# Selective scan: the product with C on GpSimd by block of 512 instead of two blocks, in half of the units

## The reference

```python
def step(hst, ins):
    dt_t, B_t, C_t, x_t = ins
    dA = jnp.exp(dt_t[:, :, None] * A)
    hst = hst * dA + (dt_t * x_t)[:, :, None] * B_t[:, None, :]
    y_t = jnp.einsum('bds,bs->bd', hst, C_t)
    return (hst, y_t)
```

## Time and profile before

| what | value |
|---|---|
| median of 3 runs | 3693.93 us (3689.43 to 3694.01) |
| profiled execution, its own time | 3693.79 us |
| its span, first to last instruction | 3691.7 us |
| TensorE busy | 3177.4 us (86%) |
| ScalarE busy | 3172.4 us (86%) |
| DVE busy | 3007.0 us (81%) |
| GpSimd busy | 2572.3 us (70%), 1578 instructions |
| mean granted TensorE clock | 0.964 of full speed |
| chain that ended last, shares | ScalarE 59%, TensorE 23%, GpSimd 11%, DVE 4% |

### The profile page before, as it was taken

The page is one execution under the profiler, slowest core; times in us unless marked ns, Lnnn a source line. Parts: engine busy times, 40 slices in busy tenths (PEclk is TensorE's granted clock), DMA queues, the critical chain, the costliest instruction groups (busy, mean ns, idle before and its releaser), DMA issues.

```text
span 3691.7 us, 55673 instructions
## 1 busy us (share of the span) xinstructions
PE 3177.4 (86%) x20898; PEld 2324.0 (63%) x20898; DVE 3007.0 (81%) x2909; ACT 3172.4 (86%) x5100; POOL 2572.3 (70%) x1578
## 2 busy tenths in 40 slices
PE   7778898888878887888798889878888898999999
PEld 3676777677767776777687777767777432222244
DVE  2797898899889988988898899889999478888341
ACT  3799999999999999999999999999999235777721
POOL 0699998899999988998998899999879100000000
PEclk9899999999999999999999999999999998999999
DMA  2011111111112111111111111112111043121000
GB/s 93 29 52 54 47 52 51 43 55 50 53 47 78 52 54 47 51 49 48 57 52 53 45 55 51 49 46 69 52 41 52 12 103 69 18 35 18 1 6 17
DMA packets 65196, 175.90 MB, mean 48 GB/s; under 512 B 13697, under 2 KB 17537, under 8 KB 64673
## 3 DMA queue, kind: packets, MB, share of 16 engines
q1 hardware_dynamic: 64930, 172.36, 15.3%
HBM read 162.83 MB, written 9.44 MB: 47 GB/s over the span
## 4 chain that ended last, share of the span: by engine, by line
ACT 59%; PE 23%; POOL 11%; DVE 4%; issue 1%; DMA 0%; SPq 0%; DVEq 0%; POOLq 0%; ACTq 0%
ACT arena L852 27%; ACT arena L859 26%; PE psum L1182 10%; POOL arena L642 10%; PE psum L1482 3%; PE psum L1471 3%; PE psum L1446 2%; DVE row_max L1135 2%; PE psum L1390 2%; PE psum L1395 1%; POOL arena L622 1%; PE psum L1415 1%; POOL carry L638 1%; DVE arena L1088 1%; ACT arena L725 1%
## 5 line engine op out<-in xcount | busy, mean ns | idle before, releaser
L642 POOL TENSOR_TENSOR arena<-arena 128x1024 f32<-128x1024 f32 x1024 | 2424.5, 2381 | 171.7 <-DVE arena L1088 127.9
L1390 PE MATMUL psum<-ident,arena 128*128 128x128 f32 x8192 | 1278.3, 280 | 323.7 <-ACT arena L852 274.6
L1390 PEld LDWEIGHTS psum<-ident,arena 128*128 128x128 f32 x8192 | 972.5, 143 | 602.1 <-ACT arena L852 385.5
L852 ACT ACTIVATE arena<-arena,bT 128x512 f32<-128x512 f32 x2048 | 1310.9, 721 | 24.2 <-PE psum L1390 24.1
L1395 PE MATMUL psum<-ident,arena 128*128 128x128 f32 x8192 | 1261.7, 278 | 80.3 <-POOL arena L642 79.4
L1088 DVE TENSOR_TENSOR_SCAN arena<-arena,psum 128x512 f32<-128x512 f32 x1024 | 1179.9, 1204 | 169.5 <-PE psum L1390 100.6
L859 ACT ACTIVATE arena<-arena,a_neg 128x512 f32<-128x512 f32 x2048 | 1312.2, 722 | 1.6 <-DVE arena L1088 1.4
L1088 DVE TENSOR_TENSOR_SCAN arena<-arena,carry,psum 128x512 f32<-128x512 f32 x1024 | 1225.1, 1260 | 95.4 <-ACT arena L859 58.4
L1395 PEld LDWEIGHTS psum<-ident,arena 128*128 128x128 f32 x8192 | 971.8, 143 | 119.2 <-POOL arena L642 118.9
L1182 PE MATMUL psum<-arena 128*128 128x512 f32 x1472 | 710.3, 606 | 14.1 <-DVE arena L968 6.2
L1182 PEld LDWEIGHTS psum<-arena 128*128 128x128 f32 x1472 | 259.9, 195 | 209.2 <-issue 200.1
(11 more groups left out here) (109 smaller groups left out, 1079.6 us busy)
## 6 DMA issues: line engine op xcount, KB each, us to landing
arena<-bc_dram SPq DMA_DIRECT2D x256, 512.0 KB, 3.6
arena<-qk_dram SPq DMA_DIRECT2D x96, 128.0 KB
qk_dram<-arena SPq DMA_DIRECT2D x12, 512.0 KB, 4.9
arena<-in_x SPq DMA_DIRECT2D x4, 512.0 KB, 10.8
arena<-in_up_w SPq DMA_DIRECT2D x1, 2048.0 KB, 12.2
out_xT<-arena SPq DMA_DIRECT2D x8, 256.0 KB, 2.2
arena<-in_mlp_w SPq DMA_DIRECT2D x3, 512.0 KB, 6.4
arena<-in_fwd_xproj_w SPq DMA_DIRECT2D x1, 1280.0 KB, 10.1
```

The source lines that it names most:

```text
L642: pool.tensor_tensor(h_now[:, f:f + NI // 2], h_now[:, f:f + NI // 2], c_row, ALU.mult)\
L852: act.activation(uT[:, w % 2, c], dtxT[:, u % 2, c], ACT.Copy, scale=bT[:, u % 2, c, st:st + 1])\
L1390: o = pe.transpose(dst[:, c * P:(c + 1) * P], uT[:, w % 2, c, f * P:(f + 1) * P], ident[:, :])
```

## The change

In the units with `hi` = 1 GpSimd multiplies each block by itself: four operations of 128x512 a state, each behind its own scan. The units with `hi` = 0 keep their copies and their two operations. Since a state now has two or four products, a function `products(w, f)` counts how many are done when block f of state w is. TensorE waits for this count ahead of every sum, where it waited ahead of every second one, and the loads of C and the first state of a unit wait for the count of a whole state.

```diff
+        def products(w, f):
+            full = {0: 2, 1: NI}
+            before = sum(DS * full[unit(u)[2]] for u in range(w // DS))
+            n = full[unit(w // DS)[2]]
+            return before + w % DS * n + (f + 1 if n == NI else f // 2 + 1)
...
                     if p >= 2:
-                        sp.wait_ge(s["prod_done"], 4 * (p - 1))
+                        sp.wait_ge(s["prod_done"], products(2 * p - 3, NI - 1))
...
-                    for k in range(2):
+                    if hi:
+                        for f in range(NI):
+                            pool.wait_ge(s["scan_done"], NI * w + f + 1)
+                            pool.tensor_tensor(h_now[:, f], h_now[:, f], c_rows[:, p % 2, w % 2], ALU.mult)\
+                                .then_inc(s["prod_done"], 1)
+                    for k in range(0 if hi else 2):
                         f = k * NI // 2
                         pool.wait_ge(s["scan_done"], NI * w + f + NI // 2)
...
             def reduce_state(w, f):
-                if f % 2 == 0:
-                    pe.wait_ge(s["prod_done"], 2 * w + f // 2 + 1)
+                pe.wait_ge(s["prod_done"], products(w, f))
...
                 if c == 0:
                     pe.wait_ge(s["skip_w_ready"], 2 * NI)
-                    pe.wait_ge(s["prod_done"], 2 * (w + 1))
+                    pe.wait_ge(s["prod_done"], products(w, NI - 1))
```

## The result

The changed kernel takes 3699.76 us in the median of 19 runs (3696.26 to 3700.85), the kernel before 3692.24 us in 19 runs beside them (3687.57 to 3694.66). The ratio is 1.0020, with a 95% interval of 1.0013 to 1.0027: slower, by 7.5 us. The forecast was no change, 3693.4 us. The profiled executions took 3693.79 and 3699.74 us, with spans of 3691.7 and 3697.7.

The account below looks back on a forecast made before the run. ScalarE was taken to set the pace in the changed units, with GpSimd close behind. Terms -1.45 + 0 + 1.0 + 0.1 = -0.35 against the profiled 3693.79 us gave 3693.4, range 3687 to 3704.

Parts of the forecast that it names:

- The price of a block: GpSimd's product of 128x512 in a chain: 1.23 us, bounds 1.17 and 1.30; 4.92 a state against 4.67.
- Full stretches of the changed units: Four changed units: GpSimd needs 319 us of a unit's 342 and stays under ScalarE's total; cost 0.
- The product dt times xs: Units 1, 3, 5, behind state 48 on GpSimd: it starts 1.0 us earlier, ScalarE's three idle times go; -1.45 us.
- From there to the unit's end: GpSimd's last 60 blocks of units 1, 3, 5 end 2.8 us later; 2.0 us of slack left; cost 0.
- Starts of changed units: Units 1, 3, 5, 7, state 0: four blocks take 4.92 where two halves take 4.67; +1.0 us.
- End of unit 7: GpSimd's last 56 blocks end 0.6 us later, four transposes instead of eight save 0.5; +0.1 us.
- The rival "slower": GpSimd becomes the late one, from 1.26 us a block; mild form 3701 to 3706, full 3726; chance 0.13.
- The rival "faster": Finer sums free TensorE sooner, 3.95 us idle at changed units' starts goes; at most 16 us, 3678; chance 0.05.

Follow-up runs that it names:

- the late wait: Changed kernel with the first state's wait for its products moved behind the skip term and made block by block: 3681.68 us, 0.9976 of the kernel before.
- its two relatives: The late wait in the kernel before, with no state split: 3691.74 us; the late wait with blocks of 512 only up to state 48: 3685.68 us.

## Why the prediction was wrong

**The price of a block** was right: 1.23 us forecast, (74.22 - 1.29) / 59 = 1.236 measured; 1296 ns for one operation against 1268 in attention. The prediction's estimate of 1.17 us, from the Trainium skill's 4497 ns (GPSIMD Engine Reference, Performance versus the Vector engine), was too low here; that figure is for an addition of 2048 elements, and a product of 2048 took 4542 ns in this trace.

**Full stretches of the changed units** were right: unit 3 takes 342 us as before, with 13 us more of GpSimd's time hidden behind ScalarE. GpSimd did not become the bound.

**The product dt times xs** had the right size: it starts about 0.9 us earlier within unit 3 (1414.86, where the unit itself starts 0.3 earlier), and ScalarE's 0.87, 0.34 and 0.24 us ahead of state 52 are gone, -1.45. The reason was incomplete, as the run with state 48 alone shows: it gave no gain.

**From there to the unit's end, cost 0**, is the step that failed. Its arithmetic held: the last product was to end at 1493.3 and ends at 1493.6, and the last sum, for which I had found 2.0 us of slack, is on time. But I followed the delay only to this one waiter. GpSimd's next work is state 0 of the next unit, 2 x 2.58 us from 1493.5 to 1498.7, and TensorE's first sum wants all of it at 1497.7. I had described exactly this wait, for the starts of the other units, and had not looked for it here. By the threshold of the forecast a block had to be over 1.26 us; it decided at less. In the profile ScalarE's idle time at the starts of units 2, 4 and 6 went from 0.96, 0.95 and 0.95 to 2.12, 3.51 and 3.32: **+6.1 us**, nearly the whole 6.0 us by which the span grew. That blocks from state 49 alone cost the full amount and blocks up to state 48 nothing in sum, and that enough idle work on GpSimd (eight memsets) does the same without any block, is shown by runs. How the 6.1 us divide into the late sum and TensorE's clock is shown in part only. The prediction had no term for the clock. It had also put the last product some 5 us behind the last scan; it ends 6.8 behind (1493.6, the scans of unit 3 at 1486.8), since the last scans come 0.9 us earlier than before.

**Starts of changed units, +1.0 us.** The waits for GpSimd grew at three of the four (0.52 to 0.79 us in unit 1, 0.36 to 0.80 in unit 5, 0.35 to 0.47 in unit 7; 0.38 instead of 0.51 in unit 3). ScalarE's idle time is 2.2 us more in sum, of which 2.0 are in unit 5, where the clock is low for longer. At the other three it changed by +0.27, -0.12 and +0.06, where +0.25 each was forecast: one of three came out, and the term as a whole was short by the clock at unit 5.

**End of unit 7, +0.1 us.** Measured +0.6: the last product ends 3.5 us behind the last scan (2.4 before), since the lag of earlier states had not run out, and TensorE's last group saves 0.43.

The sum -1.45 + 6.1 + 2.2 + 0.6 is 7.5, and the span grew by 6.0. Of the rest 0.99 us is idle time of ScalarE ahead of state 52 of unit 0, which is gone too; about 0.5 us is not accounted for. The rival "slower" named the right engine and the right stretch, the chain without a gap, but its price came from the last sums and from a threshold that did not decide. The rival "faster" said that the idle time at the start of a changed unit could go; it does not by the change. Once the wait is late 1.8 instead of 3.9 us are left, of which 1.6 are the clock and not the finer sums: with the late wait and the low clock 3.46 are left.

What stays open is why the clock stays high at all starts in the late wait with all states split and falls at some in its two relatives, behind gaps of the same 2.0 us. The length of the gap itself was not varied.

## What to carry to other kernels

When an engine that is not the bound gets slower, follow its delay to every one that waits for it, past the first waiter that is still on time: the work queued behind the delayed piece, here the next unit's first state, has a waiter of its own. A chain without a gap in an engine with slack overall is the place to look, since there every added tenth is kept until the chain ends. And at a boundary, try to put a wait behind whatever does not need it, but measure it in place: with this one wait moved the split that had cost 7.5 us gained 10.4, the same move without the split gained nothing, and most of the 10.4 came with a clock that stayed high for a reason that these runs do not show.

## What the runs showed of the hardware

Two operations in a row on GpSimd overlap by about 0.06 us also at 128x512: 1296 ns each, 1236 from start to start.

Waits of TensorE of 1.18 and 1.95 us ahead of the first sums of units 4 and 6 came with 2.6 and 2.4 us more of idle time on ScalarE. When TensorE was kept busy meanwhile the growth over the kernel before was 0.6 and 0.8 us; the granted clock over 12 us was then 1.00 at both, instead of 0.72 and 0.86. Two memsets more per unit (1.1 us of GpSimd's time) raised the median by 7.3 us over three units, while the first six had raised it by 0.8. So the same small delay was worth twice its length here in one case and little in the other.

TensorE's clock fell at starts of units behind gaps of 2.00 and 2.06 us (six of seven in the kernel before, where 0.35 to 0.51 us of waiting for GpSimd followed at units 3, 5 and 7) and stayed high behind gaps of the same length in the late wait. With blocks up to state 48 and the late wait both cases stand in one execution, and the low clock cost ScalarE 1.6 us of idle time at a changed unit's start and 0.94 at the other kind. The Trainium skill (TensorE: Matmul & The Clock Gate, Part 1) states the two levels, half and full rate, set by how busy the engine has been; the trace agrees on the levels: four transposes take 1.06 and 0.60 us, and from the start of four to the next it is 0.86 and 0.44 us (1500.72 to 1501.58, and 1506.17 to 1506.61, in the changed kernel). How busy TensorE has to be to keep the high clock no run here shows.
